# SyncE fetches two chunks of every gather pass row by row; edges laid out by tiles

## The chip, the cores and the metric

One core of a Trainium2 chip runs the kernel. Its engines are TensorE (PE; PEld is its weight load), VectorE (DVE), ScalarE (ACT), GpSimd (POOL) and SyncE (SP, which issues DMAs, waits on semaphores and signals). The metric is the time of one execution in microseconds, as the median of several runs.

## The reference, cut to what matters

A graph of 6,250 nodes and 100,000 edges, edges sorted by `dst`, goes through four blocks, each with a residual:

```python
h = relu(layernorm(x)); x = x + gcn_conv(gcn_conv(h, W1, b1), W2, b2)
      # gcn_conv: (x @ W)[src] * norm, segment_sum over dst, + b   (self-loops added)
h = relu(layernorm(x)); x = x + capsule_routing(h)
      # z = l2norm(h)[src]; three times: p = softmax(<z, u[dst]>); u = l2norm(segment_sum(z * p) + xc)
h = relu(layernorm(x)); x = x + relu(mean_over_neighbours(h)[node] @ W + b)
h = relu(layernorm(x)); m = gelu(concat(h[src], edge_attr) @ W1 + b1) @ W2 + b2
      x = x + layernorm(h + segment_sum(m, dst)) * gamma + beta
```

What is costly is `h[src]`: 100,000 rows of 128 floats (512 B each), picked in no order from a table in HBM, once for each of five passes.

## The kernel before, in words

The edges are cut into 196 chunks of 512 (the last has 256), a chunk into 4 tiles of 128 edges (the last into 2). There are seven passes over all chunks: CONV1, CONV2, CAPS1, CAPS2, CAPS3, MEAN, EDGE. Five of them gather (`GATHERS`): all but CAPS2 and CAPS3, which load again what CAPS1 saved to `z_rows`.

**Gather.** In a gather pass POOL issues one indirect DMA for each tile (line 759), 782 in all. It brings 128 rows of the pass's table into a slot. CAPS1 has 7 slots (`RING`, the tile `ring`); the other four have 14 (`FAR`), which lie in the tile `u_parts`, and there `ring` is idle. Before a chunk whose slot was used, POOL waits on `slot_free`.

**Sums.** The sum over `dst` is a staircase of 244 steps (196 chunks and 48 further blocks): a step is DVE's one-hot of `dst` (line 1374) and 4 tiles of matmuls (line 835, seen in the trace as x8 on PE) of one chunk against one block of 128 nodes, and DVE's addition. Every 4 steps a window of 4 blocks is finished: it is turned (line 796), multiplied with the weights (line 807), normed where the pass needs it, and stored as the next pass's table. A pass's first gather waits until every window of the pass before is stored.

**SyncE.** SP ties the two together. For each chunk, in order, it waits until all its tiles have landed (line 588) and adds one to `landed`, which the consumers wait for; then it waits until an older chunk (7 back with 14 slots, 3 back with 7) was used (line 595), and adds one to `slot_free` (line 597). It needs the step at which a chunk is last used, and loads 7 or 14 such numbers from SBUF into registers at a time (line 600, shown as TENSOR_LOAD). In CAPS1 it also saves each chunk to `z_rows` (line 642).

**Start.** Before the first gather DVE counts degrees and norms `x`; its last work there is `acc<-h,dinv` (line 1476), which becomes the table of CONV1.

Of the kernel before, what the change touches and what calls it, by code (L numbers as in the profile page):

```python
# [13 lines left out]
DST_ROW = CHUNK // 2  # L14
DST_ROWS = CHUNKS * CHUNK // DST_ROW
# [8 lines left out]
RING = 7  # L24
# [30 lines left out]
def tiles_before(p, j):  # L55

    ends = sum((CHUNKS - 1) % SLOTS[g] == j for g in GATHERS if g < p)
    return uses_before(p, j, GATHERS) * TILES - ends * (TILES - LAST_TILES)


def build(nc, x_in, src_in, dst_in, dst_rows_in, row_last_in, last_row_in, last_col_in, attr_rows, w1, b1, w2, b2, w_mean, b_mean,
          w_edge, b_edge, w_out, b_out, gamma, beta, out):
    fp32, bf16, i32 = mybir.dt.float32, mybir.dt.bfloat16, mybir.dt.int32
# [6 lines left out]
    with ctx:  # L70
# [118 lines left out]
        tables = {p: nc.dram_tensor(f"table{p}", [NB * P, P], fp32, kind="Internal").ap() for p in GATHERS}  # L189
        hot_rows = nc.dram_tensor("hot_rows", [STEPS, P, 2 * TILES * P], bf16, kind="Internal").ap()  # L190
# [26 lines left out]
        z_seen = sem("z_seen")  # L217
# [66 lines left out]
        ring_flat = ring[:, :, :].rearrange("p j n -> p (j n)")  # L284
        x_flat, h_flat, acc_flat = (buf[:, :, :].rearrange("p b f -> p (b f)") for buf in (x, h, acc))
# [246 lines left out]
        def _(sp):  # L532
# [5 lines left out]
            sp.dma_start(src[:, :], src_in).then_inc(src_loaded, 16)  # L538
            for tile, w in ((W1, w1), (W2, w2), (WM, w_mean), (WE, w_edge[0:P, :]), (WO, w_out)):
                sp.dma_start(tile[:, :], w).then_inc(w_loaded, 16)  # L540
# [10 lines left out]
            for half in range(FAR // RING):  # L551
                load_attr(half, half)
            sp.wait_ge(tabs_ready, 1)

            for p in PASSES:
# [21 lines left out]
                there_sems = rows_loaded if loads else rows_in  # L577

                def publish(j, q, last=False, p=p, there_sems=there_sems, loads=loads):

                    if loads:
                        sp.wait_ge(there_sems[j], (q + 1 + uses_before(p, j, (CAPS2, CAPS3))) * 16)
                    else:
                        tiles = tiles_before(p, j) + TILES
                        if last and j == (CHUNKS - 1) % SLOTS[p]:
                            tiles -= TILES - LAST_TILES
                        sp.wait_ge(there_sems[j], q * (16 * TILES) + 16 * tiles)
                    sp.sem_inc(landed, 1)  # L588

                def free(key, j, q, p=p):  # L590

                    if p == CAPS1:
                        sp.wait_ge(z_saved[j], (q + 1) * 16)
                        sp.sem_inc(z_seen, 1)
# [9 lines left out]
                def far_round(q, first, last=False, p=p):  # L604

                    c0 = q * FAR
                    for half in range(2):
                        frees = not first or half
                        if frees:
                            keys = keys_of(c0 + (half - 1) * RING, RING)  # L610
                        if p == EDGE:
                            sp.wait_ge(attr_in[half], q * 16 + 16)
                            sp.sem_inc(attr_there, RING)
                        for j in range(RING):
                            publish(half * RING + j, q, last)
                            if frees:
                                free(keys[j], None, None)
                        if p == EDGE and frees and not (last and half):
                            load_attr(1 - half, q * 2 + (1 + half))

                def round_of(q, first, last=False, p=p, loads=loads):

                    c0 = q * RING
                    keys = () if first and loads else keys_of(c0 if first else c0 - RING, RING if first else 2 * RING)
                    at = 0 if first else RING
                    for j in range(RING):
                        back = j - LAG
                        turn = q if back >= 0 else q - 1
                        there = not first or back >= 0
                        if loads:  # L630
                            if there:
                                publish(back % RING, turn)
                            if not first:
                                free(keys[at + j - RING], j, q - 1)
                            elif p == CAPS3 or j >= RING - LAG:
                                free(keys_left[j], j, CHUNKS // RING - 1, p - 1)
                            sp.dma_start(ring[:, j, :], z_rows[ds(c0 + j, 1), :, :]
                                         .rearrange("c p n -> (c p) n")).then_inc(rows_loaded[j], 16)
                        else:
                            publish(j, q, last)  # L640
                            if p == CAPS1:
                                sp.dma_start(z_rows[ds(c0 + j, 1), :, :].rearrange("c p n -> (c p) n"),
                                             ring[:, j, :]).then_inc(z_saved[j], 16)
                            if there:
                                free(keys[at + back], back % RING, turn)

                rounds = CHUNKS // SLOTS[p]
                one_round = far_round if SLOTS[p] == FAR else round_of
                one_round(0, True)
                with sp.Fori(1, rounds if loads else rounds - 1) as q:  # L650
                    one_round(q, False)
                if not loads:
                    one_round(rounds - 1, False, True)
                keys = keys_of(CHUNKS - RING, RING)
                if loads:
                    for j in range(RING - LAG, RING):
                        publish(j, rounds - 1)
                keys_left = keys
                for j in () if p in (CAPS1, CAPS2) else range(0 if loads or SLOTS[p] == FAR else RING - LAG, RING):
                    free(keys[j], j, rounds - 1)  # L660
# [13 lines left out]
        def _(pool):  # L674
# [70 lines left out]
            for n, p in enumerate(GATHERS):  # L745
# [8 lines left out]
                for c in range(CHUNKS):  # L754
                    if c >= slots:

                        pool.wait_ge(slot_free, before_this + c + 1 - slots)
                    for t in range(TILES if c < CHUNKS - 1 else LAST_TILES):
# [495 lines left out]
        def _(dve):  # L1254
# [188 lines left out]

            def nearest(q):
# [422 lines left out]
```

## Time and profile before

| | |
|---|---|
| median of 3 runs | 6134.75 us (6134.14 to 6145.96) |
| the profiled execution | span 6133.4 us, first to last instruction; only its span is given |
| busy POOL, PE, DVE, ACT | 74%, 64%, 61%, 27% |
| indirect DMAs of the five gather passes | 3910 |

Times are microseconds from the span's start unless marked ns. A row's last bracket is how long the engine sat idle before it, and what ended that: another engine, SPq (SyncE's own queue), a DMA, or "issue", where the engine waited for nothing that the profile shows. SP's instructions have durations but count as no engine's busy time.

### The profile page before, as it was taken

How to read it: one execution, taken by the hardware profiler on the slowest of the kernel's cores; microseconds unless marked ns; L12 is line 12 of the kernel's file. 1: busy time of each engine (PE TensorE's matmuls, PEld its weight loads, DVE VectorE, ACT ScalarE, POOL GpSimd, SP SyncE). 2: the span in 40 equal slices, each digit the busy share in tenths (PEclk: the TensorE clock that was granted, in tenths of full speed). 3: DMA queues.
4: the chain of work that ended last, by engine and by line, in shares of the span. 5: the costliest groups of instructions: out<-in, count | busy, mean ns of one | idle time of the engine just before them, and what ended most of it. 6: DMA issues, size and time to landing. Idle time of an engine off the chain costs nothing. (4 is left out here: it accounts for less than half of the span.)

```text
span 6133.4 us, 123500 instructions
## 1 busy us (share of the span) xinstructions
PE 3912.3 (64%) x27584; PEld 3400.1 (55%) x27585; DVE 3726.0 (61%) x9157; ACT 1638.9 (27%) x4058; POOL 4562.7 (74%) x5214
## 2 busy tenths in 40 slices
PE   1555555555555477777789989956566665666665
PEld 1544444455455366666578878845555553555553
DVE  6333333565666677777887787775555555555555
ACT  1000000112121333333455565531111113222222
POOL 6777777677777677777778888857777776777776
PEclk9666666666666688888899999977777776888887
DMA  4222222222222355555577777732222222222222
GB/s 124 68 70 68 70 69 68 62 69 68 70 68 70 103 175 171 172 170 171 169 231 248 249 226 248 249 109 69 69 69 69 70 68 54 71 71 71 69 71 95
DMA packets 447304, 697.73 MB, mean 114 GB/s; under 512 B 89485, under 2 KB 204570, under 8 KB 446282
## 3 DMA queue, kind: packets, MB, share of 16 engines
q0 software_dynamic: 127616, 263.32, 16.6%
q10 hardware_dynamic: 210816, 255.92, 12.8%
q1 hardware_dynamic: 108746, 177.24, 9.1%
q14 instruction: 98, 0.80, 0.0%
q8 instruction: 28, 0.46, 0.0%
HBM read 506.58 MB, written 189.53 MB: 113 GB/s over the span
## 5 line engine op out<-in xcount | busy, mean ns | idle before, releaser
L759 POOL DMA_INDIRECT u_parts<-table,src x3128 | 2951.6, 944 | 1063.2 <-issue 952.1
L835 PE MATMUL ps_sum<-u_parts,onehot 128*128 x2928 | 655.5, 395 | 691.6 <-SPq L588 552.2
L1374 DVE SCALAR_TENSOR_TENSOR onehot<-dst,minus_row,beside 128x512 f32<-128x512 f32 x1100 | 816.9, 744 | 365.7 <-issue 308.6
L835 PEld LDWEIGHTS ps_sum<-u_parts,onehot 128*128 128x128 f32 x2928 | 573.7, 291 | 776.2 <-issue 775.4
L759 POOL DMA_INDIRECT ring<-table,src x782 | 746.2, 954 | 264.9 <-issue 237.7
L835 PE MATMUL ps_u<-u_parts,onehot 128*128 x2928 | 535.9, 343 | 515.6 <-SPq L588 452.2
L835 PEld LDWEIGHTS ps_sum<-msg,onehot 128*128 128x128 f32 x4896 | 693.7, 213 | 306.8 <-issue 149.1
L835 PE MATMUL ps_sum<-msg,onehot 128*128 128x128 f32 x4896 | 753.9, 303 | 127.0 <-DVE msg L457 96.9
L835 PEld LDWEIGHTS ps_u<-u_parts,onehot 128*128 128x128 f32 x2928 | 473.0, 246 | 566.0 <-issue 565.0
L1669 DVE TENSOR_TENSOR zu<-ps_u,ring 128x512 f32<-128x512 f32 x732 | 502.7, 687 | 351.7 <-SPq L588 192.6
L885 PE MATMUL ps_u<-u_parts,hots 128*128 x5856 | 487.9, 235 | 56.2 <-ACT hots L1144 39.4
L913 PE MATMUL ps_u<-WE_attr,attr_t 128*128 128x512 f32 x488 | 317.2, 738 | 315.8 <-ACT attr_t L1231 303.4
L1680 DVE TENSOR_REDUCE logit<-zu 128x32 f32<-128x512 f32 x732 | 500.3, 684 | 11.0
L885 PEld LDWEIGHTS ps_u<-u_parts,hots 128*128 128x128 bf16 x5856 | 409.0, 106 | 112.2 <-issue 95.1
L954 ACT ACTIVATE wide_t<-ps_a 128x512 f32<-128x512 f32 x244 | 143.1, 587 | 1100.8 <-PE ps_a L796 1082.6
L457 POOL TENSOR_TENSOR msg<-ring,prob_n 128x512 f32<-128x512 f32 x366 | 389.1, 1063 | 55.9 <-POOL prob_n L730 48.4
L1389 DVE TENSOR_TENSOR acc<-ps_sum,acc 128x128 f32 x488 | 140.2, 287 | 427.4 <-PE ps_sum L835 425.5
L968 ACT ACTIVATE small<-small 128x4 f32<-128x4 f32 x122 | 25.0, 205 | 1104.8 <-DVE small L1351 1104.8
L1781 DVE TENSOR_TENSOR zu<-ps_u,u_parts 128x512 f32<-128x512 f32 x244 | 167.8, 688 | 234.8 <-PE ps_u L913 170.5
L1239 ACT ACTIVATE msg<-zu 128x512 f32<-128x512 f32 x244 | 152.8, 626 | 573.9 <-DVE zu L1781 426.1
L913 PEld LDWEIGHTS ps_u<-WE_attr,attr_t 128*128 128x128 f32 x488 | 89.6, 229 | 332.2 <-DVE zu L1781 191.6
L796 PE MATMUL ps_a<-ident,wide 128*128 128x128 f32 x976 | 225.2, 375 | 72.6 <-DVE wide L1739 39.5
(205 smaller groups left out, 6477.8 us busy)
## 6 DMA issues: line engine op xcount, KB each, us to landing
ring<-z_rows SPq DMA_DIRECT2D x392, 256.0 KB, 3.5
hot_rows<-hots ACTq DMA_DIRECT2D x244, 256.0 KB
hots<-hot_rows ACTq DMA_DIRECT2D x244, 256.0 KB, 3.4
z_rows<-ring SPq DMA_DIRECT2D x196, 256.0 KB, 2.1
u_parts<-table,src POOLq DMA_INDIRECT x3128, 2.5
table<-hots ACTq DMA_DIRECT2D x122, 256.0 KB
wide<-hot_rows ACTq DMA_DIRECT2D x122, 256.0 KB, 3.4
wide_t<-hot_rows ACTq DMA_DIRECT2D x122, 256.0 KB, 3.5
```

What stands on the lines that cost most here:

```text
L457: return eng.tensor_tensor(messages_at[buf].rearrange("p (c d) -> p c d", d=CAP_DIM), ring_flat[:, ds(ring_at(chunk), TILES * P)].rearrang ...
L759: nc.gpsimd.indirect_dma_start(out=slot(p, c % slots)[:, t * P:(t + 1) * P], out_offset=None, in_=tables[p], in_offset=bass.IndirectOffset ...
L796: last = nc.tensor.transpose(ps_a[:, t * P:(t + 1) * P], win_in[:, t, :], ident[:, :])
L835: last = nc.tensor.matmul(sums[k % len(sums)][:, 0:P], lhsT=(onehot[:, k % HOTS, :, :] if hots_of is None else hots_of)[:, t, :], rhs=rows ...
L885: last = nc.tensor.matmul(ps_u[(k - back) % 2][:, t * P:(t + 1) * P], lhsT=hot_pairs[at][:, 1, t * P:(t + 1) * P], rhs=parts[:, i * P:(i + ...
L913: nc.tensor.matmul(ps_u[k % 2][:, :], lhsT=attr_t[:, k % 2, :], rhs=WE_attr_flat, start=True, stop=True).then_inc(attr_mm, 1)
L954: nc.scalar.activation(win_t.rearrange("p t f -> p (t f)"), ps_a[:, :], ACT.Copy)\
L1239: nc.scalar.activation(msg[:, (k - 1) % 2, :], zu[:, (k - 1) % 2, :], ACT.Gelu)\
L1374: V.scalar_tensor_tensor(out=buffers[k % len(buffers)], in0=per_row(dst[:, ds(chunk * TILES, TILES)], [P, TILES, P]), scalar=minus_row0[:, ...
L1669: V.tensor_tensor(zu[:, one, :], ps_u[one][:, :], ring_flat[:, ds(place, TILES * P)], ALU.mult)\
L1680: V.tensor_reduce(logit[:, one, :], zu[:, one, :].rearrange("p (c d) -> p c d", d=CAP_DIM), AX, ALU.add)\
L1781: V.tensor_tensor(zu[:, one, :], ps_u[one][:, :], ring_of(EDGE)[:, ds(ring_at(chunk(1), EDGE), TILES * P)], ALU.add)\
```

## The change

Two chunks of each gather pass are no longer gathered by POOL. With 14 slots they are chunks 101 and 194, in CAPS1 chunks 100 and 194. SP fetches their 2 x 512 rows with one DMA of 512 B each, 5 or 6 in every chunk of the pass, after its work for that chunk. They go to a place that is idle (slots 0 and 1 of `ring`; in CAPS1 `msg` and `before`). When the chunk's slot is free, SP copies the 256 KB there with one DMA, and waits for that DMA where it would have waited for POOL's. The other chunks and their slots are as before.

SP needs the rows' numbers as byte offsets. They come in as a new input `staged` (2 x 1024 numbers), DVE shifts them left by 9 in place before it counts degrees, and SP loads them from SBUF into registers for 4 chunks at once (21 or 22 at a time). Two idle parts of SBUF hold them: `ring` slots 5 and 6, and `attr`. Since CAPS1 uses `ring`, its list is copied to HBM at the start and fetched back before MEAN; the first two loads of `attr` move from the start to the start of MEAN.

The gather passes of SP are now straight code, not loops, and the numbers at line 600 are loaded 7 at a time in CAPS1 too. Lastly an edge's place in its chunk changes: edge e was at partition e / 4, tile e % 4, and is now at partition e % 128, tile e / 128, so that a row's place follows from its number; `src`, `dst` and `attr` are laid out alike.

```diff
+ROW_CHUNKS = {p: 2 for p in GATHERS}
+BACK = {p: RING if SLOTS[p] == FAR else LAG for p in GATHERS}
+def load_position(p, c):
+    return c - SLOTS[p] + BACK[p]
+LISTS = 4
+LAST_FETCH = {p: load_position(p, CHUNKS - 2) - 1 for p in GATHERS}
+def rows_by(p, c):
+    return min(ROW_CHUNKS[p] * CHUNK, (c + 1) * ROW_CHUNKS[p] * CHUNK // LAST_FETCH[p])
...
+                def fetch_rows(r0, offsets, p=p):
...
+                        place = row_place(k).bitcast(u8)[row:row + 1, t * ROW_BYTES:(t + 1) * ROW_BYTES]
+                        sp.dma_start(place, table[ds(offset, ROW_BYTES)].unsqueeze(0)).then_inc(rows_staged[GATHERS.index(p) % 2][k], 16)
+                def gathered(p=p):
+                    back = BACK[p]
+                    for c in range(CHUNKS):
+                        if c % RING == 0:
...
+                            keys = tuple(keys) + tuple(keys_of(c, RING))
...
+                        if c in STAGED[p]:
+                            sp.wait_ge(staged_in_slot, 16 * staged_by(p, c))
                         else:
+                            sp.wait_ge(rows_in[c % SLOTS[p]], landed_by(p, c))
+                        sp.sem_inc(landed, 1)
+                        if p == CAPS1:
+                            sp.dma_start(z_rows[c], ring[:, c % RING, :]).then_inc(z_saved[c % RING], 16)
+                        old = c - back
+                        if old >= 0:
...
+                            free(keys[old - (c // RING * RING - (len(keys) - RING))])
+                        for k, d in enumerate(STAGED[p]):
+                            if c == load_position(p, d):
+                                sp.wait_ge(rows_staged[GATHERS.index(p) % 2][k], fetched_by(p, k))
+                                sp.dma_start(slot(p, d % SLOTS[p]), row_place(k)).then_inc(staged_in_slot, 16)
+                        r0, r1 = (rows_by(p, c - 1) if c else 0), rows_by(p, c)
+                        if c % LISTS == 0:
...
+                            offsets = offsets_of(r0, r_end) if r_end > r0 else ()
+                        fetch_rows(r0, offsets[r0 - r_list:r1 - r_list])
...
+                    if p == MEAN:
+                        sp.dma_start(far_list, row_offsets).then_inc(list_copied, 16)
+                        for half in range(FAR // RING):
+                            load_attr(half, half)
+                        sp.wait_ge(list_copied, 32)
...
                 for c in range(CHUNKS):
+                    if c in STAGED[p]:
+                        continue
                     if c >= slots:
...
+            dve.wait_ge(list_loaded, 32)
+            for listed in (far_list, caps_list):
+                V.tensor_scalar(listed, listed, ROW_SHIFT, None, ALU.logical_shift_left).then_inc(list_scaled, 1)
...
-        return padded.reshape(CHUNKS, P, -1).transpose(1, 0, 2).reshape(P, -1)
+        return padded.reshape(CHUNKS, TILES, P).transpose(2, 0, 1).reshape(P, -1)
```

POOL's gathers of CONV1 and CONV2 (`u_parts`) and of CAPS1 (`ring`), before:

```order
L759 DMA u_parts<-table,src 128x128 x1564
L759 DMA ring<-table,src 128x128 x782
```

and now:

```order
L865 DMA u_parts<-table,src 128x128 x1548
L865 DMA ring<-table,src 128x128 x774
```

Eight fewer in each pass, nothing else on POOL.

SP in CONV1, chunks 7 to 10, before (the ALU rows compute the step to wait for; `rows_in` is the landing of a slot's tiles):

```order
L600 TENSOR_LOAD key_row [waits rows_in0,rows_in1,rows_in2,rows_in3,rows_in4,rows_in5,rows_in6]
L595 REGISTER_ALU [waits rows_in7]
L595 REGISTER_ALU
L595 REGISTER_ALU [waits step_summed,rows_in8]
L595 REGISTER_ALU
L595 REGISTER_ALU [waits step_summed,rows_in9]
L595 REGISTER_ALU
L595 REGISTER_ALU [waits step_summed,rows_in10]
```

and now:

```order
L662 TENSOR_LOAD key_row
L657 REGISTER_ALU [waits rows_in7]
L657 REGISTER_ALU
L704 DMA ring<-table 1x512 [waits step_summed]
L704 DMA ring<-table 1x512 x5
L657 REGISTER_ALU [waits rows_in8]
L657 REGISTER_ALU
L692 TENSOR_LOAD ring [waits step_summed]
L704 DMA ring<-table 1x512 x5
L657 REGISTER_ALU [waits rows_in9]
```

Between a chunk's wait for its use and the next chunk's wait for its landing now stand 5 or 6 DMAs, and at every fourth chunk a register load.

DVE between the norms of `x` and its count of degrees, now (`ring` and `attr` hold the lists):

```order
L1411 SCALAR_TENSOR_TENSOR small<-small 128x52 [waits chain]
L1552 TENSOR_SCALAR ring<-ring 1x1024 [waits list_loaded]
L1552 TENSOR_SCALAR attr<-attr 1x1024
L1558 TENSOR_SCALAR onehot,below<-acc,node_id 128x256 [waits near_in0]
```

and before:

```order
L1305 SCALAR_TENSOR_TENSOR small<-small 128x52 [waits chain]
L1448 TENSOR_SCALAR onehot,below<-acc,node_id 128x256 [waits near_in0]
L1448 TENSOR_SCALAR onehot,below<-acc,node_id 128x256 x3
```

Two operations on one partition come in.

## Rows read from the trace of the kernel before

**Rows 1.** The page: span, then busy time, share, instructions; busy tenths in 40 slices
```profile
span 6133.4 us, 123500 instructions
...
POOL 6777777677777677777778888857777776777776
```

**Rows 2.** Windows, all engines, each gather pass: length, busy, PE clock, DMA share
```profile
97.70:1073.70 976.00, 521.25 (x2661) 470.91 (x2662) 355.13 (x665) 35.82 (x60) 737.87 (x782) 0.69 0.26 68
1088.80:2064.80 976.00, 542.81 (x2659) 484.73 (x2660) 581.51 (x1667) 187.04 (x473) 737.85 (x782) 0.66 0.26 68
2091.50:3075.80 984.30, 696.04 (x5820) 580.44 (x5820) 768.14 (x1965) 369.88 (x772) 746.20 (x782) 0.82 0.54 172
4099.20:5075.30 976.10, 596.43 (x3358) 540.89 (x3359) 519.72 (x1490) 176.56 (x414) 737.96 (x782) 0.74 0.26 68
5106.90:6082.90 976.00, 654.01 (x3136) 484.09 (x3136) 547.49 (x1197) 250.86 (x593) 737.87 (x782) 0.82 0.25 69
```

**Rows 3.** Source L759: durations in ns; what ended its idle time (us, times)
```profile
L759 POOL DMA_INDIRECT u_parts<-table,src x3128: 938/944/980, 97.8 to 6081.9; - x196
...
  issue: 1189.8, 3904
...
  SPq L597: 0.3, 1
```

**Rows 4.** Timeline of POOL, end of CONV1 and start of CONV2
```profile
1072.72 0.94 POOL L759 DMA_INDIRECT u_parts<-table,src  x1 [0.30 <-issue]
1088.85 0.94 POOL L759 DMA_INDIRECT u_parts<-table,src  x1 [15.18 <-DMA table<-h]
```

**Rows 5.** Timeline of PE, last steps of CONV1
```profile
1068.18 1.15 PE L835 MATMUL ps_sum<-u_parts,onehot 128*128 x8
1069.17 1.06 PE L807 MATMUL ps_b<-W,wide_t 128*128 128x128 f32 x8
1073.08 1.15 PE L835 MATMUL ps_u<-u_parts,onehot 128*128 x8 [2.86 <-SPq L588]
1076.22 2.07 PE L835 MATMUL ps_u<-u_parts,onehot 128*128 x8 [1.98 <-SPq L588]
```

**Rows 6.** Windows of PE there: length, busy, granted clock
```profile
1068.00:1071.00 3.00, 2.17 (x18) 1.00 0.24 68
1076.00:1079.00 3.00, 2.07 (x8) 0.50 0.29 87
```

**Rows 7.** Timeline of PE, end of CONV2, of CAPS1 and of EDGE
```profile
2064.18 1.92 PE L835 MATMUL ps_u<-u_parts,onehot 128*128 x8 [1.30 <-SPq L588]
...
3058.46 1.16 PE L835 MATMUL ps_sum<-msg,wide 128*128 128x128 f32 x8
...
3062.12 1.16 PE L835 MATMUL ps_sum<-msg,wide 128*128 128x128 f32 x8
...
6078.92 1.05 PE L835 MATMUL ps_sum<-msg,onehot 128*128 128x128 f32 x8
...
6081.19 1.05 PE L835 MATMUL ps_sum<-msg,onehot 128*128 128x128 f32 x8
```

**Rows 8.** Source L642, 2200 to 3000: SP's saves in CAPS1, ns min/median/max
```profile
L642 SPq MOVE z_rows<-ring x160: 29/29/38, 2204.3 to 2998.2; - x160
L642 SPq DMA_DIRECT2D z_rows<-ring x160: 327/332/333, 2204.4 to 2998.2; - x160
```

**Rows 9.** Timeline of SP, the start
```profile
1.29 0.32 SPq L534 DMA_DIRECT2D last_row<-in_last_row  x1
1.66 0.35 SPq L535 DMA_DIRECT2D last_col<-in_last_col  x1
...
12.52 0.75 SPq L546 DMA_DIRECT2D BE<-in_L_gnn_b  x1
```

**Rows 10.** Source L600: register loads in CONV1 (7 values), CAPS3 (14), CAPS1 (14)
```profile
L600 SPq TENSOR_LOAD <-key_row x23: 922/1468/1950, 204.3 to 973.2; - x23
...
L600 SPq TENSOR_LOAD <-key_row x42: 1167/2874/2894, 3203.6 to 3899.0; - x42
...
L600 SPq TENSOR_LOAD <-key_row x23: 1378/3442/4056, 2205.5 to 2974.5; - x23
```

**Rows 11.** Waits of DVE in CAPS1, 2200 to 3000: us in total, times, longest
```profile
DVE zu L1669 <- SPq L588: 145.5, 102, 2.1
```

**Rows 12.** Timeline before the first gather, DVE, then POOL
```profile
35.57 0.26 DVE L1420 TENSOR_SCALAR tmp_row<-last_row 1x196 int32<-1x196 int32 x1
...
40.40 0.48 DVE L1436 TENSOR_SCALAR minus_row<-minus_block 128x256 f32<-128x256 f32 x1
...
88.13 2.89 DVE L1476 TENSOR_TENSOR acc<-h,dinv 128x2048 f32<-128x2048 f32 x2
...
97.77 0.94 POOL L759 DMA_INDIRECT u_parts<-table,src  x1 [25.75 <-DMA table<-acc]
```

**Rows 13.** The page: DMA queue of POOL's gathers; and POOL early in CAPS1
```profile
q0 software_dynamic: 127616, 263.32, 16.6%
...
2102.08 1.86 POOL L759 DMA_INDIRECT ring<-table,src  x1 [0.30 <-issue]
```

More of the change, by code:

```diff
@@ L576, in _, with publish_loaded, free @@
                           .then_inc(h_in[q], 16)
[L577 to L587, printed above, removed]
+                def publish_loaded(j, q, p=p):
+                    sp.wait_ge(rows_loaded[j], (q + 1 + uses_before(p, j, (CAPS2, CAPS3))) * 16)
                     sp.sem_inc(landed, 1)
[L590 to L594, printed above, removed]
+                def free(key, p=p):
                     sp.wait_ge(msg_ready if p in (CAPS1, CAPS2, CAPS3) else step_summed,
@@ L602, in keys_of @@
                         max_val=STEPS - 1, skip_runtime_bounds_check_because=BY_TABLE)[1]
[L604 to L619, printed above, removed]
@@ L621, in round_of, with loaded_round @@
-                def round_of(q, first, last=False, p=p, loads=loads):
+                def loaded_round(q, first, p=p):
                     c0 = q * RING
-                    keys = () if first and loads else keys_of(c0 if first else c0 - RING, RING if first else 2 * RING)
-                    at = 0 if first else RING
+                    keys = () if first else keys_of(c0 - RING, 2 * RING)
                     for j in range(RING):
                         back = j - LAG
[L628 to L638, printed above, removed]
-                        else:
-                            publish(j, q, last)
-                            if p == CAPS1:
[L642 to L654, printed above, removed]
+                        if not first or back >= 0:
+                            publish_loaded(back % RING, q if back >= 0 else q - 1)
@@ L655, in _ @@
                 if loads:
+                    loaded_round(0, True)
+                    with sp.Fori(1, CHUNKS // RING) as q:
+                        loaded_round(q, False)
                     for j in range(RING - LAG, RING):
[L657 to L660, printed above, removed]
+                        publish_loaded(j, CHUNKS // RING - 1)
@@ new lines, in _ @@
+                    keys_left = keys_of(CHUNKS - RING, RING)
+                else:
+                    if p in (CONV1, MEAN):
+                        sp.wait_ge(table_stored, 16 * len(CUTS) * (1 if p == CONV1 else 2))
+                    else:
+                        sp.wait_ge(rows_stored, 16 * WINDOWS * ((CONV2, CAPS1, EDGE).index(p) + 1))
+                    if p == CONV1:
+                        sp.wait_ge(list_copied, 16)
+                    if p == MEAN:
[3 more added lines that the diff above has]
+                        sp.wait_ge(list_copied, 32)
+                    keys_left = gathered()
@@ L662, in _ @@
+                if p not in (CAPS1, CAPS2):
+                    for j in range(0 if loads else RING - BACK[p], RING):
+                        free(keys_left[j])
             sp.wait_ge(rows_stored, 16 * WINDOWS * 4)
```

87 lines of the change are left out of this document (77 added, 10 removed).

## The prediction

> **What bounds the kernel now.** I read the page first. No engine is near 100%, but POOL has the largest share and its slices hardly dip between passes [rows 1], so the question is what stands between its instructions. Next the windows, one for each gather pass: each holds 782 indirect DMAs and lasts 976.0 us, whatever PE (521 to 696 us busy), DVE (355 to 768) or the DMA share (0.26 to 0.54) do in it; only CAPS1 takes 984.3 [rows 2]. Then the source line: a gather is 944 ns long, and of POOL's idle time before gathers 1189.8 us in 3904 pieces are "issue", 0.3 us each, waited for by nothing; a wait for a free slot cost 0.3 us once [rows 3]. So a gather costs 976.0 / 782 = 1.248 us from start to start, POOL runs without a break, and the five passes last 4888 of 6133 us. Between two passes stands a tail: CONV1's last gather begins at 1072.72 and CONV2's first at 1088.85, released by the store of the table [rows 4]. A microsecond saved on POOL is thus a microsecond of the pass, unless the tail grows or another engine steps in.
>
> **What goes: 40 gathers.** 8 in each pass, 8 x 1.248 = 9.98 us, 49.9 us in five passes. No cover is lost, for nothing else is on POOL there. The other gathers keep their form and size. The new layout of the edges changes which edges share a tile, but not the number of rows or matmuls, and `src` is in no order in either layout: nothing.
>
> **What the end of a pass gives back.** Chunk 101 is early enough for its consumers to catch up. Chunk 194 is the last but one. At the end of CONV1 PE's steps for chunks 193, 194 and 195 begin at 1068.18, 1073.08 and 1076.22, the last two released by SP [rows 5]. With the change 193 lands 4.99 us earlier (1063.19), 194 lies ready, and 195 lands 9.98 us earlier (could start at 1066.24). In these 3.05 us PE must do the steps of 193 and 194 and a product between them. At granted clock 1.00 (2.4 GHz) they take 1.15, 1.06 and 1.15 us, at 0.50 (1.2 GHz) 2.07 each [rows 5, 6]: 3.2 to 6.7 us with their gaps. So the pass ends 9.8 to 6.3 us earlier; I take 8, as two of the three rows before are at the upper level. In CONV2 the norms of the last window but one lie behind the step of 194 (2064.18 [rows 7]), which moves by 5.6 to 7.8 us: 7. MEAN has a second turn and product in each window, which the rows shown don't cover; by the same reckoning 5 to 8, taken 6.5. In EDGE a step with its other products takes 6081.19 - 6078.92 = 2.3 us [rows 7], two of them 4.5 against 3.05, or about 9 at the lower level: 4 to 8.5, taken 7.5. In CAPS1 a step takes 3062.12 - 3058.46 = 3.7 us [rows 7], two 7.3 against 3.05: 5.7 is left, minus what SP may be late (below): 3 to 8, taken 5. Sum 8 + 7 + 5 + 6.5 + 7.5 = 34.0 us.
>
> **What SP takes on.** 1024 DMAs in 186 to 189 chunks of a pass, 21.6 for four chunks, which last 16 x 1.248 = 20 us. No row DMA is in the trace. The nearest by its address from a register is the save of CAPS1: 29 ns of MOVE and 332 ns of DMA, with two gaps of 40 to 50 ns, as between the DMAs at the start, 0.44 us [rows 8, 9]; the nearest in shape is `last_row`, one partition, 0.37 from start to start (1.66 - 1.29). A DMA behind a backlog took 0.75 us [rows 9]. Bounds 0.37 and 0.79; I take 0.44. A register load takes 1468 ns for 7 values and 2874 for 14: 0.2 us a value, so 4.5 us for 22. The minima, 922 and 1167 ns, come at every fourth load, where the first number's place divides by 4 [rows 10]; by these 22 values take 1.5. A far pass has half of its lists at such a place, CAPS1 a quarter, and its loads are 3442 / 2874 = 1.2 times as long. Per four chunks of a far pass: rows 9.5, list 3.0, keys 0.8, waits and ALU 1.2, together 14.5 of 20 us. CAPS1: rows 9.5, list 4.5, keys 0.9, saves 1.8, waits 1.4, together 18.1 of 20. SP stays off the path in both, with 0.70 and 0.53 us per row as the points at which it would not.
>
> The Trainium skill (Runtime: NRT & Kernel Launch, Instruction fetch mechanics) puts such loads at about 200 ns a register even in bulk. The trace agrees at three loads of four and not at the fourth; by the rule alone a far pass would come to 16 of 20 us and CAPS1 to nearly 19, and the forecast would be the same.
>
> What waits behind these DMAs is the next chunk's signal. At a list of 4.5 us with its rows (2.6) and the rest, chunk c + 1 is signalled some 3 us late, then SP catches up. POOL doesn't feel it: its slot was freed chunks ago [rows 3]. DVE in CAPS1 does, as it waits for SP at 102 chunks already [rows 11]; it then lags by these 3 us and keeps pace. The last full list is read at chunk 184, so little of it is left at the end of a pass. The copies of 256 KB, the wait for the rows and the wait for the copy are 7 (in CAPS1 4) chunks ahead: nothing. At the start of MEAN the list, `attr` and the wait lie beside POOL's first chunk (5 us and landing): nothing; without that cover 3 us.
>
> **What the start pays.** Two shifts of 1024 numbers on one partition stand on DVE's way to the first table: its last multiplication ends at 91.0, the table is stored and POOL starts at 97.77 [rows 12]. An integer shift of 196 took 0.26 us with its fixed part, 1.3 ns an element, and 256 floats 0.48, 1.9 ns [rows 12]; 1024 elements take 0.7 (if the fixed part is most of it) to 1.9. Taken 1.0 each: 2.0 us later, between 1.4 and 3.8. The loads of the lists are long done by then.
>
> **Sum.** 34.0 - 2.0 = 32.0 us less than the span of 6133.4; the runs' median stands 1.35 above the span, as the work around it is unchanged: 6134.75 - 32.0 = 6102.7, 6103 us. Its own range, with every bound at either end, is 6091 to 6113.
>
> **Rivals.**
> (a) Full gain. The consumers absorb the last burst and the tails stay as long as now: 49.9 - 2 = 48 us, 6087. For it speaks CONV1's end at the upper level (9.8 of 9.98); against it EDGE's and CAPS1's steps. 7%.
> (b) The second chunk gains almost nothing: the tails swallow all of it, and late signals as well. Then 5 x 5 - 2 = 23 us, 6112, and down to 6122 where SP is 2 us late in each. For it: the norms of CONV2 and MEAN stand in line behind the last steps. 12%.
> (c) SP binds, first in CAPS1. A row there at 0.58 us instead of 0.44 makes 0.58 x 21.6 + 8.6 = 21.1 us for four chunks, 49 times 1.1 = 56 us more, minus 27 gained elsewhere: 6164. It decides from 0.56 us a row; at 0.79, the backlog's price, far passes would take 22 us for four chunks too and the kernel 6700. For it: 90% load in CAPS1, and nobody has shown such a row. Against: the saves kept to 327 to 333 ns amid that pass's traffic, and a row of 512 B leaves no backlog. 12%.
> (d) The rows get in the way of the gathers. All go to one partition each, so perhaps to a single DMA engine. POOL's packets take 16.6% of 16 engines, 127616 of them [rows 13], 128 ns each; 1024 more on one engine are 131 of 976 us, 0.26 becomes 0.39, in CAPS1 0.54 becomes 0.68 [rows 2]. That only lengthens landings, which have slack. But early in CAPS1 a gather took 1.86 us beside SP's loads of `h` [rows 13]; if each of 3870 got 1% (12 ns) longer, 48 us would be gone and the kernel at 6134 or above. Against: 944 ns in CAPS1 as elsewhere once the loads are over. 6%.
>
> [...] Nothing in this trace shows which engine a packet ran on. [...]
>
> **How the numbers follow.** Forecast 63%, (a) 7, (b) 12, (c) 12, (d) 6. The range takes in (a) and most of (b): 6085 to 6124. A measurement of this kernel tells some 0.2% (12 us) from no change. Faster: the forecast, (a), most of (b): 81%. Within 0.2%: the rest of (b), half of (d): 7%. Slower: (c) and the rest of (d): 12%.
>
> **What will show it.** Five windows with 774 gathers and 966 us each; 976 with fewer gathers is (d), more than that with POOL waiting for `slot_free` is (c). SP's row DMAs at 0.33 to 0.36 us, its list loads in two kinds, 1.5 and 4.5 us. The last three steps of CONV1 back to back on PE, and the time from a pass's last gather to the next pass's first 2 to 5 us longer than before (16.1 in CONV1). The first gather near 99.8. Wrong would be: a period of a gather other than 1.25, a tail longer by 5 us or more outside CAPS1, or POOL idle for slots.

## The result, and the profile after

| | before | after |
|---|---|---|
| median | 6135.56 us (4 runs, 6134.14 to 6145.96) | 6097.38 us (4 runs, 6096.41 to 6100.63) |
| span of the profiled execution | 6133.4 us | 6094.7 us |

The ratio is 0.9939, 95% interval 0.9927 to 0.9950: 38.2 us less, where 32 were forecast. A later measurement of the same instructions (e6) gave 6098.10 against 6135.32. But on three other chips the kernel before takes 7500 to 7618 us; the changed kernel ran on one of these, and there it is slower than before, by 0.8%. The experiments had to explain both.

The page after, in the columns of [rows 1]:

```profile
span 6094.7 us, 132845 instructions
...
POOL 6777777677777677777778888857777775777775
```

The windows of the five gather passes, as in [rows 2]:

```profile
98.90:1065.10 966.20, 516.89 (x2645) 469.15 (x2646) 353.95 (x664) 35.70 (x60) 730.35 (x774) 0.70 0.26 70
1079.90:2046.00 966.10, 541.40 (x2645) 484.77 (x2646) 579.11 (x1662) 185.32 (x469) 730.34 (x774) 0.66 0.26 70
2075.70:3049.10 973.40, 668.39 (x5784) 556.67 (x5785) 760.32 (x1954) 366.27 (x765) 737.64 (x774) 0.85 0.55 174
4071.10:5037.20 966.10, 593.66 (x3336) 539.84 (x3336) 519.68 (x1489) 173.94 (x412) 730.27 (x774) 0.73 0.26 70
5071.90:6038.00 966.10, 645.56 (x3104) 477.84 (x3105) 544.79 (x1186) 249.23 (x591) 730.31 (x774) 0.81 0.25 71
```

Every far pass has 774 gathers and lost 9.9 us, CAPS1 10.9. The windows' sum falls from 4888.4 to 4837.9, 50.5 us. The source line of the gathers, against [rows 3]:

```profile
L865 POOL DMA_INDIRECT u_parts<-table,src x3096: 940/944/980, 99.0 to 6037.0; - x194
...
  issue: 1174.8, 3853
...
  SPq L659: 3.7, 12
```

A gather is still 944 ns, and POOL waited 3.7 us for slots in all. The first gather starts later [rows 12], and DVE's two shifts are the two 0.67 us rows:

```profile
56.00 0.67 DVE L1552 TENSOR_SCALAR ring<-ring 1x1024 int32<-1x1024 int32 x1
56.60 0.67 DVE L1552 TENSOR_SCALAR attr<-attr 1x1024 int32<-1x1024 int32 x1
...
98.95 0.94 POOL L865 DMA_INDIRECT u_parts<-table,src  x1 [26.48 <-DMA table<-acc]
```

What SP does now, source lines 704 (rows) between 300 and 1000 us and 692 (lists) in all passes, ns min/median/max:

```profile
L704 SPq MOVE ring<-table x776: 29/29/38, 300.3 to 996.0; - x194
L704 SPq DMA_DIRECT2D ring<-table x776: 227/228/390, 300.4 to 996.0; - x194
```
```profile
L692 SPq TENSOR_LOAD <-ring x188: 924/2315/5229, 105.3 to 5992.4; - x188
L692 SPq TENSOR_LOAD <-attr x48: 1742/5582/6170, 2086.4 to 3023.8; - x48
```

And its waits from 300 to 1000 us (us in total, times, longest):

```profile
SPq L720 <- DMA u_parts<-table,src: 249.6, 114, 3.3
```

SP waited 249.6 of 700 us for gathers, so it is full for 64%, 12.9 of every 20 us. Before, in the same stretch, it waited 628.1: the 776 rows with their lists cost 378.5 us, 0.49 us a row. In CAPS1, from 2200 to 2900 us, it waited 125.9 of 700, so it is full for 16.4 of 20 us.

**Between the passes**, from the last gather's end to the next pass's first (us):

| | CONV1 | CONV2 | CAPS1 to MEAN | MEAN | EDGE to the end |
|---|---|---|---|---|---|
| before | 15.2 | 26.8 | 1023.5 | 31.7 | 50.6 |
| after | 14.9 | 29.8 | 1022.1 | 34.8 | 56.7 |
| the changed kernel again (e6) | 14.0 | 29.5 | 1020.6 | 36.7 | 57.3 |

The last row is another execution of the same instructions: differences under 2 us in this table are not told from chance by one trace.

CONV1's end on POOL [rows 4], and on PE [rows 5]:

```profile
1079.92 0.94 POOL L865 DMA_INDIRECT u_parts<-table,src  x1 [14.88 <-DMA table<-h]
```
```profile
1064.48 1.15 PE L941 MATMUL ps_sum<-u_parts,onehot 128*128 x8
1065.47 1.06 PE L913 MATMUL ps_b<-W,wide_t 128*128 128x128 f32 x8
1066.36 1.06 PE L941 MATMUL ps_u<-u_parts,onehot 128*128 x8
1067.85 1.15 PE L941 MATMUL ps_u<-u_parts,onehot 128*128 x8 [0.42 <-SPq L720]
```

The steps run nearly back to back as forecast, but all with the durations of the upper clock level (1.06 and 1.15 us a step, [rows 5, 6]), the last too, which took 2.07 before. It had to wait for SP's signal (0.42 us). So PE catches up entirely and nothing is given back.

In CONV2 PE's last step and the turn of the last window, before, then after:

```profile
2067.41 2.07 PE L835 MATMUL ps_u<-u_parts,onehot 128*128 x8 [1.31 <-SPq L588]
2071.77 1.11 PE L796 MATMUL ps_a<-ident,wide 128*128 128x128 f32 x4 [2.29 <-DVE wide L1516]
```
```profile
2049.03 1.95 PE L941 MATMUL ps_u<-u_parts,onehot 128*128 x16
2055.96 1.12 PE L902 MATMUL ps_a<-ident,wide 128*128 128x128 f32 x4 [4.98 <-DVE wide L1626]
```

The last step ends 4.77 us after POOL's last gather before (which ended at 2064.71), and 5.02 after: 0.25 us more. The rest of the 2.9 us is in DVE, for whose `wide` the turn waits. The norms of the last windows end with `hots<-hots,ps_c`. Before, then after:

```profile
2063.62 0.69 DVE L1538 TENSOR_TENSOR hots<-hots,ps_c 128x512 f32<-128x512 f32 x1
2071.03 0.69 DVE L1516 TENSOR_TENSOR wide<-h,beside 128x512 f32 x1 [0.34 <-DVE h L1389]
```
```profile
2049.93 0.69 DVE L1648 TENSOR_TENSOR hots<-hots,ps_c 128x512 f32<-128x512 f32 x1
2055.22 0.69 DVE L1626 TENSOR_TENSOR wide<-h,beside 128x512 f32 x1 [0.34 <-DVE h L1495]
```

Before, the norms of the last window but two were done 0.4 us before POOL's last gather ended (2063.62 + 0.69 against 2064.71). After, they are done 4.7 us behind it (2050.62 against 2045.96). This slide of 5.1 us is the time of the four gathers of chunk 194 (4.99 us), which no longer stand between the landing of chunk 193 and POOL's end. The last window's `wide` then starts 9.3 us behind POOL's end instead of 6.3, which is the 2.9 us.

EDGE gives back most, 6.2 us. PE after, from POOL's last gather (6037.02 to 6037.96) on, against the last of [rows 7]:

```profile
6038.24 1.05 PE L941 MATMUL ps_sum<-msg,onehot 128*128 128x128 f32 x8
...
6039.99 1.05 PE L941 MATMUL ps_sum<-msg,onehot 128*128 128x128 f32 x8
...
6042.26 1.05 PE L941 MATMUL ps_sum<-msg,onehot 128*128 128x128 f32 x8
...
6045.24 1.16 PE L941 MATMUL ps_sum<-msg,onehot 128*128 128x128 f32 x8 [1.92 <-ACT msg L1345]
...
6047.46 1.16 PE L941 MATMUL ps_sum<-msg,onehot 128*128 128x128 f32 x8 [0.17 <-ACT msg L1345]
```

Five steps are left when POOL is done, where two were left before (6084.17 and 6086.76, POOL's end 6082.83). EDGE's sums follow the landing by some steps, and a window's turn and product stand among them.

CAPS1 gave back nothing, it gained 1.4 (3.0 in e6). Chunk 195 was signalled 4.9 us after POOL's end before and is signalled 3.2 us after it now. SP was not late with either: it stood idle until the rows had landed. Before, one more register load of 1.89 us followed; now there is none, as all keys of a gather pass are read inside its straight code. So SP's first load for CAPS2 is issued 4.1 us behind POOL's end instead of 7.6. DVE's first `zu` of CAPS2, before, then after:

```profile
3086.18 0.69 DVE L1669 TENSOR_TENSOR zu<-ps_u,ring 128x512 f32<-128x512 f32 x1 [3.02 <-SPq L588]
```
```profile
3059.22 0.68 DVE L1779 TENSOR_TENSOR zu<-ps_u,ring 128x512 f32<-128x512 f32 x1
```

DVE's last `zu` of CAPS1 did slide, as forecast, from 5.1 to 8.0 us behind POOL's end. But before, DVE then stood idle for 3.0 us until CAPS2's first chunk was there; now it goes straight on, and starts on CAPS2 10.2 us behind POOL's end where it started 10.4. The slide was taken up by that wait.

### The profile page after: what moved, and what is told of

It reads as the page before. It is cut to its first block and busy times, and to the rows that moved or that the text cites. A ratio compares the mean times of both kernels' runs of the same rounds, so it can differ in the third digit from the quotient of the medians.

```text
span 6094.7 us, 132845 instructions
## 1 busy us (share of the span) xinstructions
PE 3875.0 (64%) x27584; PEld 3373.1 (55%) x27585; DVE 3724.8 (61%) x9159; ACT 1637.2 (27%) x4058; POOL 4523.9 (74%) x5174
## 3 DMA queue, kind: packets, MB, share of 16 engines
q10 hardware_dynamic: 210816, 255.92, 12.9%
## 5 line engine op out<-in xcount | busy, mean ns | idle before, releaser
L865 POOL DMA_INDIRECT u_parts<-table,src x3096 | 2921.3, 944 | 1057.8 <-issue 942.9
```

Of the source, the lines that this page charges most:

```text
L865: nc.gpsimd.indirect_dma_start(out=slot(p, c % slots)[:, t * P:(t + 1) * P], out_offset=None, in_=tables[p], in_offset=bass.IndirectOffset ...
```

## The experiments

All but e6, e7 and e10 ran on chips on which the kernel before takes 7500 to 7618 us. They were three chips. There is no trace of the kernel before on any of them; e1's is the nearest. The ratios are to before on the same chip. A chip with before at 6135 us is called quick here, the others slow.

**e10: SP's instructions without the transfers** (quick).

```diff
-  sp.dma_start(place, table[...]).then_inc(rows_staged[...][k], 16)
+  for _ in range(2): sp.sem_inc(stepped_on, 1); sp.wait_ge(stepped_on, n)
...
```

All gathers stay, no chunk is copied, and the loads of the lists are gone too, since nothing reads them.

> SyncE's added instructions without its transfers: GpSimd gathers all 782 blocks of each pass as before, and in place of each of the 5120 row transfers (a register instruction and an issue) SyncE runs two semaphore instructions that wait for nothing; the register loads of the lists are gone too. Where GpSimd sets the pace: both theories 1.2 us over before (two shifts at the start). Where SyncE is late (before at about 7500 to 7600 us, and the kernel with rows fetched but unused 1.4% over it), Theory A (what is slow there is the delivery of instructions: 0.70 us for one where it takes 0.03 us elsewhere, whatever the instruction does): the 10240 added instructions cost most of what the row transfers did, 1.008 to 1.014 of before. Rival B (the transfers or the loads of the lists are what costs): 1.000 to 1.004.

6132.82 against 6135.32, 0.9995 [0.9986, 1.0005]. The far passes keep 975.8 us. It was 2.5 us under before, not 1.2 over: the first gather came at 98.88, 1.1 later, but CAPS1's end is 3.3 us shorter (1020.25 for 1023.53). Of these some 2 us are the register load that fell away: SP's first load for CAPS2 is issued 5.5 us behind POOL's end instead of 7.6. So the straight code on SP costs nothing here, and the new layout, which this run has too, neither. Whether the slow chips' cost is of instructions or of transfers, it couldn't tell.

**e6: CAPS1's lists twice** (quick).

```diff
+  if p == CAPS1 and r_end > r0:
+      offsets = offsets_of(r0, r_end)
```

> The changed kernel with CAPS1's lists loaded into registers twice, which adds 5.3 us of SyncE's time to each four chunks of CAPS1 and nothing elsewhere. It asks how near SyncE is to being the bound there. Where GpSimd sets the pace, Theory (SyncE has 18 of 20 us full in CAPS1, so that 5.3 us more put it at 23 to 24 us): CAPS1's gathers take 60 to 180 us longer, and the time is 6160 to 6280. Rival (SyncE's time in CAPS1 has cover left, because part of it is spent in waits that the added loads fill): at most 10 us over the changed kernel, 6097 to 6107. Where SyncE is already the bound (before at 7500 to 7600), the 48 added loads, 5.6 us each, show in full: 250 us over what the changed kernel takes there.

6098.10, 0.9940 [0.9924, 0.9957]; but it tests neither theory. Its trace has as many instructions and list loads as the changed kernel's (236): the compiler dropped the first, unused load. It stands as a second measurement of the changed kernel: 37.2 us less than before. How far SP is from binding in CAPS1 here is left to its waits.

**e7: three chunks in the far passes, the last at 180** (quick).

```diff
-ROW_CHUNKS = {p: 2 for p in GATHERS}
...
-LISTS = 4
-LAST_FETCH = {p: load_position(p, CHUNKS - 2) - 1 for p in GATHERS}
+ROW_CHUNKS = {p: 3 if SLOTS[p] == FAR else 2 for p in GATHERS}
+LISTS = 2
+LAST_FETCH = {p: load_position(p, CHUNKS - 16) - 1 for p in GATHERS}
...
-    return min(ROW_CHUNKS[p] * CHUNK, (c + 1) * ROW_CHUNKS[p] * CHUNK // LAST_FETCH[p])
+    return min(ROW_CHUNKS[p] * CHUNK, (c + 1) * ROW_CHUNKS[p] * CHUNK // LAST_FETCH[p] // 4 * 4)
```

> Three chunks of each far pass (66, 123 and 180) and two of CAPS1 (93 and 180) row by row, all done by position 180, with lists that begin at a whole multiple of four numbers so that no register load takes 4.6 us. Where GpSimd sets the pace: 16 gathers more go (4 passes by 4), 20 us, and with 15 chunks left behind the last staged one less is given back at the ends: Theory A 6065 to 6085 on a chip where the kernel before takes 6135. Rival: SyncE, with 1536 rows in 180 chunks at 0.33 us, 11.3 us of every 20 us for four chunks beside the 10 us it had, binds the far passes: 6100 or more. Where SyncE or the delivery of its instructions already sets the pace (before at 7500 to 7600), the added 2048 rows cost more than two chunks do: a ratio of 1.02 to 1.04.

6072.03, 0.9896 [0.9880, 0.9913]: the best version here, 26.1 us under e6 on the same chip. The window of CONV1 (the other far passes have 961.1 us too), and the list loads:

```profile
99.20:1060.30 961.10, 524.01 (x2658) 476.38 (x2659) 354.35 (x664) 35.82 (x60) 726.50 (x770) 0.69 0.27 71
```
```profile
L692 SPq TENSOR_LOAD <-ring x344: 972/1201/2189, 105.6 to 5897.1; - x172
L692 SPq TENSOR_LOAD <-attr x88: 534/1291/1942, 2073.7 to 2940.5; - x88
```

Theory A's size was right. Each gather removed is worth 1.248 us again (770 in 961.1), and SP does not bind: it waited 137.3 us of 700 for gathers in CONV1. And with no staged chunk among the last slots, the end of CONV2 is 26.1 us (before 26.8, after 29.8), MEAN's 32.6 (31.7, 34.8). In CONV2 DVE's window is done before POOL's end again, at 2036.51 against 2036.88:

```profile
2035.82 0.69 DVE L1648 TENSOR_TENSOR hots<-hots,ps_c 128x512 f32<-128x512 f32 x1
```

This fits a staged chunk near the end as the cause of what is given back in CONV2 and MEAN. It is not shown alone, for e7 also changed the number of chunks and where the lists begin; in CONV2 the slide of DVE's window by the four gathers of 194 speaks for it. EDGE's end did not shorten (59.5 us): there five steps of PE are behind POOL's end in e7 too (6013.97 to 6023.46, POOL's end 6012.27), so the staged chunk near the end is not what puts them there. The cause in EDGE stays open.

**e9: the changed kernel on a slow chip.**

> The changed kernel itself, beside the kernel before on the same chip. Where the pace of a pass is that of GpSimd (a gather starts every 1.248 us with no wait for a slot between them, before's passes take 976 us), both theories expect what the first pair showed: 38 us less than before. Where the passes are slower than GpSimd's gathers (before at 7603 us, its passes 1137 to 1435 us, GpSimd waiting for slots that SyncE has yet to publish), the theories differ. Theory A, ten gathers less a pass are worth something only where a gather is what the pass waits for: there the ten are worth nothing and SyncE's added instructions cost time, so a ratio between 1.00 and 1.02. Rival B, a gather less is worth its 1.248 us on any chip: 38 us less, a ratio of 0.995.

7571.46 against 7513.69, 1.0077 [1.0060, 1.0094]. Its trace has the very instructions of the quick one. Waits of SP from 300 to 1000 us, all of them, and windows of the same 700 us on the quick chip, then here:

```profile
SPq L659 <- PE ps_u L941: 1.0, 2, 0.7
SPq L659 <- PE ps_sum L941: 0.4, 1, 0.4
```
```profile
300.00:1000.00 700.00, 378.77 (x1951) 344.62 (x1952) 258.41 (x485) 26.59 (x45) 529.21 (x561) 0.69 0.27 70
```
```profile
300.00:1000.00 700.00, 332.71 (x1593) 302.52 (x1592) 211.83 (x398) 21.49 (x36) 430.30 (x457) 0.62 0.22 57
```

SP never waits for a landing, 457 gathers start where 561 did, and POOL waits for slots: 1390.9 us in 458 waits over the run, 3.7 us on the quick chip. That wait is not the change's, though: in e1, the kernel before on another slow chip, it is 1338.5 us in 434. SP's row instructions there:

```profile
L704 SPq MOVE ring<-table x634: 2/29/1396, 299.7 to 999.3; - x159
L704 SPq DMA_DIRECT2D ring<-table x634: 3/228/1397, 301.1 to 1000.0; - x159
```

The medians are the quick chip's, but the longest is 1.4 us. Between neighbouring rows in this stretch the mean distance is 0.78 us (0.33 on the quick chip), and half of the distances are over 0.5. Over the run 1275 of SP's register and semaphore instructions last 0.6 to 0.8 us, none on the quick chip. SP is the bound of this far pass, as Theory A had it (1.00 to 1.02; Rival B's 0.995 is out): this is the prediction's rival (c) on another chip, beyond its own point for a far pass, 0.70 us a row. It does not come first in CAPS1, as (c) had it: from 2700 to 3400 us, in CAPS1, SP waited 127.5 us of 700 for DVE.

**e1: the kernel before with the new edge layout** (slow).

```diff
-  padded.reshape(CHUNKS, P, -1).transpose(1, 0, 2).reshape(P, -1)
+  padded.reshape(CHUNKS, TILES, P).transpose(2, 0, 1).reshape(P, -1)
...
```

> The kernel before with the new place of an edge in its chunk and nothing else. Theory (the gain is 40 gathers that POOL no longer issues): no change, 6135 within 6 us, a gather still every 1.248 us. Rival (the layout itself gives part of the 38 us): 6125 or less.

7599.36 against 7603.05, 0.9994 [0.9981, 1.0007]: the layout costs nothing (on a quick chip e10 is the nearest test), and its trace shows what the kernel before does on such a chip. Window, and waits of PE, in the same 700 us:

```profile
300.00:1000.00 700.00, 335.27 (x1648) 301.89 (x1649) 218.02 (x416) 22.71 (x38) 452.07 (x478) 0.65 0.23 59
```
```profile
PE ps_sum L835 <- issue: 220.0, 61, 8.5
PE ps_a L796 <- issue: 103.9, 31, 8.8
```

Only 478 gathers here too, and PE sits idle 324 us for nothing that the profile shows (0.8 us before line 835 in before's trace on the quick chip). In PE's queue 524 register and semaphore instructions last 0.6 to 0.8 us where they else take 0.03 to 0.1. POOL isn't the bound of the pass even before the change: PE is. SP waits 581 of the 700 us, so its rows could lie beside PE's work until they reach its pace.

**e8: rows fetched but not used** (slow): all gathers stay, no copy.

```diff
+USED = {p: [] for p in GATHERS}      # asked in place of STAGED by POOL and by SP's waits
-  sp.dma_start(slot(p, d % SLOTS[p]), row_place(k)).then_inc(staged_in_slot, 16)
```

> The cost side alone: SyncE fetches every row of the two chunks as in the changed kernel, but they stay unused: GpSimd gathers all 782 blocks of each of the five passes as before, and no staged chunk is copied to its slot. Theory (the gathers removed are all of the gain, and SyncE's row transfers lie beside GpSimd's work): where GpSimd sets the pace the passes keep 976 us, and the time is before plus the two shifts at the start, +1.2 us (6137). Rival (the row transfers hold up the gathers or the saves of results, and part of the gain pays for that): passes 1 to 3 us longer each, 6141 to 6151. Where SyncE sets the pace of the passes, its 1024 added issues a pass at 0.33 us, 340 us in all, can show in full or in part.

7613.50, 1.0142 [1.0120, 1.0165]: the rows, with all else that the change has, cost 100 us there. With the gathers gone and the copies in (e9, the same chip) it is 42 us less, near the 50 us that 40 gathers are worth on a quick chip. So Rival B's size is not ruled out for the gathers alone, only for the whole change.

**e2 and e3: one chunk a pass** (slow), early (101 or 100, 512 rows by then) or late (194).

```diff
-ROW_CHUNKS = {p: 2 for p in GATHERS}
+ROW_CHUNKS = {p: 1 for p in GATHERS}
```
with, for e2 alone:
```diff
-LAST_FETCH = {p: load_position(p, CHUNKS - 2) - 1 for p in GATHERS}
+LAST_FETCH = {p: load_position(p, 101 if SLOTS[p] == FAR else 100) - 1 for p in GATHERS}
```

> The changed kernel with one chunk of each pass for SP, the early one alone (101, in CAPS1 100), its rows at the same rate as now until chunk 92. Theory (a chunk is worth 4 gathers, 5.0 us, and only the late one, 194, gives back, at the end of the pass): 25 us from five passes, some 2.5 us from the end of CAPS1, 0.6 us paid at the start: 6109; the times between a pass's last gather and the next pass's first as before, 26.8 us for CONV2 and 31.7 for MEAN. Rival (SP's new code and not the late chunk makes these longer, 12 us in CONV2, MEAN and EDGE): they stay long, 6121.

> The changed kernel with the late chunk alone (194), 512 rows over the whole pass, half as many row DMAs in each chunk. Theory: 25 us from the gathers, 2.5 from the end of CAPS1, minus 12 given back at the ends of CONV2, MEAN and EDGE, minus 0.6 at the start: 6121, and these three ends longer by 2.9, 3.1 and 6.2 us as in the changed kernel. Rival (what is given back grows with SP's DMAs): half of it, 6115.

e2 7651.77, 1.0061 [1.0048, 1.0073]; e3 7566.19, 0.9946 [0.9934, 0.9958]. The numbers expected were for a quick chip and are not tested. They differ in the place of the chunk and in the rate: e2 fetches 5 to 6 rows a chunk in the first half, e3 2.8 all the way. SP's waits for e3 sum to 122 us of 700 in the stretch where e9 has 1.4:

```profile
SPq L659 <- PE ps_sum L941: 64.0, 25, 5.0
SPq L659 <- remote: 49.6, 26, 4.8
SPq L659 <- PE ps_u L941: 8.1, 2, 5.0
```

SP has cover left. But it is not shown that the 20 gathers less make e3 faster. Against e1, on the same chip, its four far windows are together 2.6 us longer (4687.6 for 4685.1), though each has 4 gathers less, and CAPS1's is 27.7 us shorter (1407.4 for 1435.1), out of 33.9 us between the two spans. In CAPS1 SP's loop became straight code and its key loads went from 14 to 7 numbers; which of these, or the 4 gathers, gives the 27.7 us no run separates. So where PE sets the pace of a far pass, four gathers less in it show no gain; this rests on one trace of each kernel, and e1's ten runs span 54 us.

**e4 and e13: two chunks, done by 180** (slow, one kernel on two chips).

```diff
-LAST_FETCH = {p: load_position(p, CHUNKS - 2) - 1 for p in GATHERS}
+LAST_FETCH = {p: load_position(p, CHUNKS - 16) - 1 for p in GATHERS}
```

> The changed kernel with the second chunk at 180 in place of 194 (the first then falls at 93 or 94), all rows fetched by chunk 172 and so 9% denser. Theory (the last chunks come in a burst that the consumers can't take): the consumers catch up before the end, the ends of CONV2, MEAN and EDGE are as short as before (26.8, 31.7, 50.6 us), 12 us less than the changed kernel: 6085. Rival (SP's lateness makes the ends longer): no gain, 6097, or more since SP has more to do in each chunk.

> The changed kernel with its two chunks at 94 and 180 (93 and 180 in CAPS1) in place of 101 and 194: the same 774 gathers a pass, the same number of rows, only the second staged chunk is not among the last slots of the pass. Theory A (what the changed kernel gives back at a pass's end comes from the staged chunk among the last three, whose steps reach TensorE in a burst while the last gathers run): gather windows stay at 966 us, the ends of CONV2 and MEAN go back to the lengths of before (29.8 to about 26.5 us, 34.8 to about 32.5), the time is 6088 to 6093. Rival B (a pass that gathers for 10 us less has its TensorE that much less far, wherever the chunks lie): the ends stay, 6096 to 6099. On a chip where the kernel before takes 7500 to 7600: 1.02 of it, as measured there once.

7773.66, 1.0218 [1.0204, 1.0231], and 7669.81, 1.0212 [1.0185, 1.0238]: one kernel gives the same ratio on two chips. Its rows are fetched by position 172 and no longer 186, 6.0 a chunk instead of e9's 5.5; e9, on a third chip, has 1.0077. What e13 was to tell, the position's part of e7's shorter ends, needs a quick chip and stays open.

**e12 and e11: three chunks everywhere, and four with three in CAPS1** (slow). Edits as in e7, with `{p: 3 for p in GATHERS}` and `{p: 4 if SLOTS[p] == FAR else 3 ...}`.

> Three chunks row by row in all five gather passes, by position 180 (the earlier kernel had three in the four far passes and two in CAPS1, 6072.03 us). Four gathers less in CAPS1. There, between 2200 and 2900 us, SyncE still waited 165 us of 700 for gathers with two chunks; a third adds 2.84 rows a chunk, 398 rows and 131 us in that stretch, and some 10 us of list loads: 20 us of cover are left. Theory A: CAPS1's gathers take 5 us less (969.4), the time is 6067, in any case 6062 to 6071. Rival: SyncE binds in CAPS1 already (its issues of 256 KB saves come in bunches): 6075 to 6110. On a chip where the kernel before takes 7500 to 7600: over 1.01 of it.

> Four chunks row by row in each far pass (51, 94, 137, 180), three in CAPS1. It is there to pass the point from which SyncE binds. With three chunks SyncE still waited 107 us of 700 in a far pass; a fourth adds 398 rows by 0.33 us, 131 us, and some 14 us of list loads: 38 us too much in 700. Theory A: a far pass is SyncE's until position 180, 900 us of gathers become about 949, so that its gathers take 985 to 1010 us where three chunks took 961, and the time is 6160 to 6270, slower than before though 78 gathers less are issued. Rival B (a gather less is worth its 1.248 us, SyncE runs ahead and its lateness is taken up by the slots): 956 us a far pass, 6047 in all. On a chip where the kernel before takes 7500 to 7600: over 1.03 of it.

7939.76, 1.0579 [1.0561, 1.0596], and 8151.23, 1.0846 [1.0828, 1.0864]. Both are as expected for such a chip (over 1.01, over 1.03); what was asked of a quick one stays open. The same window, e12 then e11:

```profile
300.00:1000.00 700.00, 313.18 (x1468) 285.62 (x1468) 196.41 (x365) 19.70 (x33) 397.55 (x421) 0.62 0.20 54
```
```profile
300.00:1000.00 700.00, 308.05 (x1411) 277.55 (x1411) 188.96 (x353) 19.10 (x32) 381.28 (x405) 0.60 0.19 52
```

Across the slow chips the gathers in these 700 us fall with the rows fetched for each chunk: 478 (no rows, e1), 474 (2.8, e3), 457 (5.5, e9), 421 (8.9, e12), 405 (11.9, e11). They stand for three chips (e1 and e3 one, e9 one, e12 and e11 one). In the first two SP still waits, in the others hardly or not.

## Why the prediction was right, and where it wasn't

**The bound and the gathers: right.** POOL's pace held at 944 ns and 1.248 us; 50.5 us went from the windows (49.9 said). CAPS1 lost 1.0 more: ten of its gathers took over 1.2 us, together 7.3 us above 944 ns each, where before twelve did, with 8.4.

**The start: 1.2 us, not 2.0.** A shift took 0.67 us, just below the 0.7 given as the lower end, and 1.0 was taken. The first gather came 1.2 us later, below the range of 1.4 to 3.8.

**Given back at the ends: 10.5 us in all, not 15.9.** From the table: CONV1 gained 10.1 (8 said), CONV2 6.9 (7), CAPS1 with its window 12.4 (5), MEAN 6.9 (6.5), EDGE 3.7 (7.5). In CONV1 the clock was at its upper level for every step, as I had left open. In CONV2 the size was right, but the reason (PE's step of 194) was the smaller part: DVE's window took it. In EDGE I took two steps to be behind POOL; five were, so the term was mis-sized by 3.8 us. EDGE's tail grew by 6.2 us, and a tail longer by 5 or more outside CAPS1 was one of the prediction's own signs of being wrong: for EDGE it was. In CAPS1 the term was mis-sized by 7.4. It took the slide of the last steps, and lateness of SP on top, as lost; but DVE had a wait of 3.0 us there, behind CAPS2's first chunk, which took up the slide, and that chunk came sooner, since a register load had gone. The straight code alone gave some 3 us of this (e10). The sum, 39.9 - 1.2 = 38.7 us, is that by which the span fell. It is only 6.7 us off the 32.0 forecast, and part of that closeness is luck: CAPS1 (7.4 too small) and EDGE (3.8 too large) missed in opposite directions, and CAPS1's gain has a part that the prediction had not seen.

**SP's rows: in cover, cheaper than taken.** 0.33 us each (0.44 taken, 0.37 the lower bound), and 12.9 of 20 us in a far pass (14.5), 16.4 in CAPS1 (18.1). List loads come in two kinds, as read from [rows 10]: in the far passes 22 values take 1.8 us (median) where the first number's place divides by 4, and 4.6 where it does not (1.5 and 4.5 said); in CAPS1 2.3 and 5.7. With lists cut at multiples of four, e7 has medians of 1.2 and 1.3 us for its shorter ones.

**The rivals.** (a) and (b) lie on either side of 6097. (d) is out: no gather got longer, though each row did come as a packet of its own: the page counts 120205 packets of 512 B to 2 KB after and 115085 before, 5120 more for 5120 rows. Which DMA engines they ran on is not shown. (c) did not happen on the chip of the prediction, and did on e9's: its condition, 0.70 us a row in a far pass, was met there by 0.78. (Its 6700 us at 0.79 us a row is a slip: by its own terms, 22.1 and 25.7 us for four chunks, it comes to about 6800.) The prediction gave (c) 12% by the price of an issue alone; that the price depends on the chip wasn't in it, and nothing in one trace of before could show it.

**Open:** why instructions take 0.7 us there. Data operations, gathers and transfers last as long as elsewhere, and the long ones are register, semaphore and issuing instructions on SP, PE, DVE and ACT. That may point to the supply of instructions, but no run tests it: e10, which bears on it, was measured on a quick chip only. The Trainium skill (Runtime: NRT & Kernel Launch, Instruction fetch mechanics) has the fetch mostly hidden in sequential code: the quick chips' traces agree, with no such instruction on SP. If the 1275 of e9, all in SP's straight code, are waits for the fetch, the slow chips do not agree; that they are is not shown.

## What to carry to other kernels

Where one engine's queue runs without a break, an instruction less is worth its start-to-start time; but look at every engine's last work at the end of a stage, not at TensorE's alone: a piece that comes early among the last ones pushes the work before it behind the end, unless something waits there anyway. Where another engine sets the pace, that worth can't be counted on: four gathers less in a far pass showed no gain in e3. An idle queue is a budget: price it in its own instructions per unit of work, and name the price at which it binds. Keep distance from that point, since a price read on one chip (0.33 us a row) was more than doubled on another (0.78), and the same change went from 0.6% faster to 0.8% slower.

## What the runs showed of the hardware

- One program, two kinds of chip: before takes 6135 us on some, 7500 to 7618 on others, with a gather at 944 to 947 ns on both, and with many single register and semaphore instructions of 0.7 us in place of 0.03 to 0.1. Why is open.
- A DMA of one row (512 B) costs SP's queue 228 ns, with its register instruction 0.33 us from start to start; one of 256 KB over 128 partitions costs 332 ns.
- A register load of 22 values from SBUF takes 1.8 us in a far pass where its first number's place is a multiple of four, and 4.6 us (medians) where it is two past one.
- A load into registers that nothing reads is dropped when the kernel is built: doubling a cost needs a look at the count of instructions.
